# Two quantised feed-forward layers: tokens kept in SBUF, bias rows made in place, ScalarE normalises layer 0, w2a loaded early, new layer 0 orders

## Reference

```python
def layernorm_adapter(x, lang):            # per batch item, weights picked by lang
    h = relu(x @ W1[lang] + b1[lang])      # 256 -> 64
    v = x + h @ W2[lang] + b2[lang]        # 64 -> 256
    n = (v - mean(v)) * rsqrt(var(v) + 1e-5)
    return n * gamma[lang] + beta[lang]
def bitlinear(x, W, b):                    # ternary weights, 8 bit tokens
    ws = clip(mean(|W|), 1e-5); Wq = clip(round(W / ws), -1, 1) * ws
    s = clip(max(|x|, axis=-1), 1e-5);  xq = round(x * 127 / s) * s / 127
    return xq @ Wq.T + b
x = x + bitlinear(gelu(bitlinear(layernorm_adapter(x), W1a, b1a)), W2a, b2a)   # layer 0, 256 -> 1024 -> 256
y = x @ cwl[subject].T + bias[subject]                                         # layer 1
h = depthwise_conv3(bit_linear(y, W1b)) ; x = x + bit_linear(silu(h), W2b)
```

## Time and profile before

| | |
|---|---|
| three runs | 339.78, 340.76, 341.88 us; median 340.76 |
| profiled execution | 339.32 us, span of its trace 337.5 us |
| busy in the span | DVE 290.4 us (86%), PE 271.0 (80%), POOL 268.2 (79%), ACT 222.6 (66%) |
| DMA | 53.12 MB, of it 8.39 MB written to HBM |

### The profile page before, as it was taken

How to read it: one execution, slowest core, us unless ns; L and a number is a source line. 1 busy time by engine, 2 the same in 40 slices (tenths; PEclk the granted TensorE clock), 3 DMA queues, 4 the chain that set the end, 5 groups by cost and what they waited for, 6 DMA issues and landing times.

```text
span 337.5 us, 6487 instructions
## 1 busy us (share of the span) xinstructions
PE 271.0 (80%) x1643; PEld 182.5 (54%) x1668; DVE 290.4 (86%) x635; ACT 222.6 (66%) x339; POOL 268.2 (79%) x443
## 2 busy tenths in 40 slices
PE   5728696897998979899868688897979889686755
PEld 5303353362555546467636467785766667464632
DVE  0427999999999999987699899999999999999651
ACT  4237689897667666562436896778768687777650
POOL 2407999998989898875899899998989899898410
PEclk9875799999799999999989999799999999979995
DMA  7896416696889798568570055667675667267883
GB/s 226 255 338 227 135 35 142 173 192 154 206 177 212 197 252 177 123 147 155 163 223 2 1 125 102 160 155 194 148 187 136 156 149 143 55 155 95 204 139 80
DMA packets 97003, 53.12 MB, mean 157 GB/s; under 512 B 74165, under 2 KB 90301, under 8 KB 96966
## 3 DMA queue, kind: packets, MB, share of 16 engines
q1 hardware_dynamic: 95078, 51.43, 63.5%
q10 hardware_dynamic: 1888, 1.27, 1.4%
HBM read 27.51 MB, written 8.39 MB: 106 GB/s over the span
## 4 chain that ended last, share of the span: by engine, by line
issue 28%; POOL 24%; DVE 23%; PE 13%; DMA 5%; SPq 3%; ACT 2%; DVEq 1%; POOLq 0%
POOL mid L755 7%; PE banks L1197 3%; POOL raw_all L762 3%; DVE amy L969 3%; DMA q1T<-r 3%; POOL xb L735 3%; DVE xb L987 2%; PE banks L1183 2%; DMA raw_all<-in_w2a 2%; PE banks L1314 2%; DVE am L930 2%; DVE raw_all L994 2%; DVE xb L963 2%; DVE zg L899 2%; POOL r L708 2%
## 5 line engine op out<-in xcount | busy, mean ns | idle before, releaser
L762 POOL TENSOR_TENSOR raw_all<-raw_all,mid 128x1024 f32<-128x1024 f32 x32 | 63.6, 1999 | 0.0
L602 ACT ACTIVATE banks<-xb,taps 128x512 f32<-128x512 f32 x64 | 43.6, 689 | 22.9 <-DVE xb L987 22.8
L542 ACT ACTIVATE g<-banks,dqz 128x1024 f32<-128x1024 f32 x32 | 35.4, 1107 | 22.2 <-POOL r L708 18.7
L755 POOL TENSOR_SCALAR mid<-xb,taps,convb 128x512 f32<-128x512 f32 x64 | 48.9, 771 | 0.9 <-DVE xb L987 0.9
L708 POOL TENSOR_SCALAR r<-g,qs 128x1024 uint16<-128x1024 f32 x32 | 36.2, 1133 | 12.1 <-DVE qs L942 12.0
L994 DVE SCALAR_TENSOR_TENSOR raw_all<-xb,taps,banks 128x512 f32<-128x512 f32 x64 | 45.7, 738 | 0.0
L1314 PE MATMUL banks<-tern,q1T 128*128 128x256 bf16 x256 | 35.7, 286 | 10.9 <-DMA q1T<-r 6.1
L987 DVE TENSOR_TENSOR xb<-banks,dqb 128x512 f32<-128x512 f32 x64 | 42.7, 683 | 1.8 <-PE banks L1288 1.8
L1183 PE MATMUL banks<-tern,qT 128*128 128x512 bf16 x117 | 37.4, 395 | 5.1 <-DVE tern L853 3.0
L1288 PE MATMUL banks<-yT,tern 128*128 128x512 bf16 x114 | 32.8, 392 | 9.8 <-DVE raw_all L994 4.8
L1000 DVE TENSOR_REDUCE am<-g 128x1 f32<-128x1024 f32 x32 | 38.8, 1212 | 1.7 <-ACT g L608 1.7
(11 more groups left out here) (113 smaller groups left out, 582.2 us busy)
## 6 DMA issues: line engine op xcount, KB each, us to landing
xr<-in_x SPq DMA_DIRECT2D x8, 512.0 KB, 4.7
x_after_layer<-x SPq DMA_DIRECT2D x16, 256.0 KB, 2.9
x<-x_after_layer SPq DMA_DIRECT2D x8, 512.0 KB, 3.7
xr<-x_after_layer SPq DMA_DIRECT2D x8, 512.0 KB, 3.8
out_y<-o SPq DMA_DIRECT2D x32, 128.0 KB, 2.0
xT<-in_xT SPq DMA_DIRECT2D x4, 512.0 KB, 4.8
x2T<-in_xT SPq DMA_DIRECT2D x4, 512.0 KB, 3.9
wl<-in_cwl SPq DMA_DIRECT2D x8, 256.0 KB, 3.6
```

The lines of the kernel that those rows point to most:

```text
L602: act.activation(bank(BANK_U[g % 3]), apad[:, f, 2:S + 2], ACT.Copy, scale=taps[:, f, 2:3]).then_inc(p_last, 1)
L755: pool.tensor_scalar(mid[f // 2 % 2][:, f % 2, :], apad[:, f, 1:S + 1], taps[:, f, 1:2], convb[:, f:f + 1], ALU.mult, ALU.add).then_inc(p_ ...
L762: pool.tensor_tensor(c[:, 2 * q:2 * q + 2, :], c[:, 2 * q:2 * q + 2, :], mid[q % 2][:, :, :], ALU.add).then_inc(p_sum, 1)
```

## The change

- Tokens stay in SBUF: `xs` holds all 8 items. `load_tokens` writes them there, `residual` adds b2 in place after `add_adapted` has read them, `final1` writes its result in place, layer 1's `transpose_x` and `final2` read it there, `final2` writes the output there, and `store2` sends it. `store1`, the token load of `load2` and `load_residual` are gone, and so are the waits of `final1` and `final2` for stores. `y`, `ry` and `apad` of layer 1 get memory of their own.
- The bias rows: b1 is loaded three times as rows of `b1row`, and ACT and DVE make the three bf16 parts in place (`bias_leading`, `bias_rest`, `bias_middle`, `bias_last`). No DRAM round trip.
- The norm: POOL makes `nratio` = -mean * rstd for a pair, ACT writes `zg` = xx * rstd + nratio (two 256 column Identity activations), and DVE multiplies by gamma and adds beta in one 512 column instruction each (`gain`, `shift`).
- `split_scales` has 4 instructions in place of 7; the transposed scale block `qc` is 128 wide in place of 9.
- `load_weights(1)` is issued before the loads of item 1; `load_weights(2)` and `(3)` go to SP's slot 3; small constants go to the end of SP's opening list; `adapter_in` no longer waits for the load of `cb1`, nor the identities for all constants.
- New orders of layer 0 on all five engines (ACT's, SP's and DVE's shown below).

```diff
+            load_weights(1)
             sp.dma_start(ids_sb[:, B:2 * B], t["ids1"]).then_inc(s_ids, 16)
...
+            def bias_leading():
+                act.wait_ge(s_wsc, 2)
+                act.wait_ge(s_ldb1, 48)
+                act.activation(bias9b[:, :], b1row[:, :], ACT.Copy, scale=iws[:, 0:1]).then_inc(s_b1, 1)
+                act.wait_ge(s_b1, 1)
+                act.activation(b1row[:, :], b1row[:, :], ACT.Copy, scale=iws[:, 0:1]).then_inc(s_b1, 1)
+            def normalise(b, p):
+                act.wait_ge(s_nratio, pair(b, p))
+                wait(act, s_z, pair(b, p - 1))
+                for k in range(2):
+                    ins = act.activation(zg[:, k, :], xx[p][:, k, :], ACT.Identity, scale=rstd[p][:, k:k + 1],
+                                         bias=nratio[p][:, k:k + 1])
+                ins.then_inc(s_norm, 1)
...
+            def negative_ratio(b, p):
+                pool.wait_ge(s_rstd, pair(b, p))
+                pool.wait_ge(s_nmean[p], b + 1)
+                wait(pool, s_norm, pair(b - 1, p))
+                pool.tensor_tensor(nratio[p][:, :], nmean[p][:, :], rstd[p][:, :], ALU.mult).then_inc(s_nratio, 1)
...
             def add_adapted(b, p):
                 dve.wait_ge(s_admm, pair(b, p))
                 dve.wait_ge(s_ldx[b % 2], 16 * (b // 2 + 1))
-                wait(dve, s_zg, pair(b - 1, p))
-                wait(dve, s_ssq, pair(b - 1, p))
+                wait(dve, s_norm, pair(b - 1, p))
...
+            def gain(b, p):
+                dve.wait_ge(s_norm, pair(b, p))
+                dve.wait_ge(s_ldgb[b % 2], 32 * (b // 2 + 1))
+                dve.tensor_tensor(zg[:, :, :], zg[:, :, :], gam[b % 2][:, :].unsqueeze(1).to_broadcast([P, 2, D]),
+                                  ALU.mult).then_inc(s_zg, 1)
+            def shift(b, p):
                 dve.wait_ge(s_zg, pair(b, p))
                 wait(dve, s_rz, pair(b - 1, p))
+                dve.tensor_tensor(z[p][:, :, :], zg[:, :, :], bet[b % 2][:, :].unsqueeze(1).to_broadcast([P, 2, D]),
+                                  ALU.add).then_inc(s_z, 1)
```

More of the change, by code:

```diff
@@ L183, in build_program @@
         s_rz = sem("s_rz")
[L184 removed]
+        s_split = sems("s_split", 3)
         s_qc = sem("s_qc")
@@ L203, in build_program, with tokens @@
         s_colsum = sem("s_colsum")
[L205 to L211, removed]
+        def tokens(b):
+            return xs[:, PAIR * b:PAIR * (b + 1), :, :].rearrange("p n a d -> p (n a) d")
         wl1 = [sb(f"wl1_{k}", [P, KD, D]) for k in range(2)]
@@ L1023, in final2 @@
                                          op0=ALU.mult, op1=ALU.add).then_inc(p_o[k], 1)
             def slot1(s):
-                on(inverse1, s - 3, 2)
+                on(inverse1, s - 3, 1)
+                on(final1, s - 4, 2)
+                on(absmax1, s - 3, 2)
+                once(s, 0, weight_scale, 0)
+                on(inverse_z, s - 2, 1)
+                on(scale1, s - 3, 2)
+                on(gain, s - 1, 0)
+                on(inverse1, s - 3, 2)
+                on(add_adapted, s, 0)
@@ L1027, in slot1 @@
+                on(shift, s - 1, 0)
+                on(negative_mean, s, 0)
+                on(final1, s - 4, 3)
+                once(s, B + 2, linear, 0, 0)
                 on(absmax1, s - 3, 3)
-                on(scale_z, s - 1, 0)
+                once(s, 2, weight_scale, 2)
+                on(absmax_z, s - 1, 0)
                 on(scale1, s - 3, 3)
-                on(add_adapted, s, 0)
-                on(inverse1, s - 3, 3)
-                on(inverse_z, s - 1, 0)
                 on(final1, s - 3, 0)
@@ L1045, in slot1 @@
-                once(s, B + 2, inverse_y, 0)
+                on(absmax1, s - 2, 0)
+                once(s, B + 2, scale_y, 0)
+                on(scale_z, s - 1, 0)
+                once(s, B + 2, inverse_y, 0)
+                on(scale1, s - 2, 0)
+                once(s, 0, bias_rest)
+                once(s, 1, weight_scale, 1)
+                on(inverse_z, s - 1, 0)
+                once(s, 3, weight_scale, 3)
+                on(inverse1, s - 2, 0)
+                on(add_adapted, s, 1)
@@ L1046, in slot1 @@
+                on(gain, s - 1, 1)
                 on(final1, s - 3, 1)
-                on(add_adapted, s, 1)
-                on(inverse1, s - 2, 0)
+                on(shift, s - 1, 1)
+                once(s, 1, ternary, 0)
+                once(s, 0, bias_last)
                 on(absmax1, s - 2, 1)
                 on(absmax_z, s - 1, 1)
-                on(centre, s, 0)
-                on(final1, s - 3, 2)
                 on(scale1, s - 2, 1)
                 on(scale_z, s - 1, 1)
-                on(inverse1, s - 2, 1)
@@ L1056, in slot1 @@
-                on(inverse_z, s - 1, 1)
-                on(absmax1, s - 2, 2)
-                once(s, 1, ternary, 0)
-                on(normalise, s, 0)
-                on(final1, s - 3, 3)
-                once(s, B + 1, linear, 0, 0)
-                on(scale1, s - 2, 2)
-                once(s, 1, weight_scale, 2)
-                on(absmax_z, s, 0)
-                once(s, 0, weight_scale, 1)
             def seam():
```

330 lines of the change are left out of this document (135 added, 195 removed).

## The result

The change makes the kernel slower: median 347.93 us (346.81 to 348.65, four runs) against 340.48 for the kernel before on the same chip, a ratio of 1.022, interval 1.019 to 1.026. I had forecast 327, with 319 to 335 around it. The profiled execution took 347.77 us with a span of 346.0, so 8.5 us more span than the 337.5 of before.

What follows compares the result with a forecast made beforehand. DVE was taken to set the pace in both layers, with PE close behind in layer 0. Gains of 7.5 (start), 1 (slots 2 to 4), 3.7 (full slots) and 1 (tail) took 339.3 to 326.1; median 327, range 319 to 335.

Steps and rivals of the forecast that it cites:

- the part on the norm: Layer 0 slots: four 512 column DVE instructions replace eight of 256, so DVE's slot goes from 15.4 to 14.4 us.
- ACT's cover: Layer 0: four more activations take ACT from 10.3 to 12.1 us of a 14.4 us slot, without lengthening a full slot.
- My price of 496 ns: ACT's two added pairs of 256 column activations a slot, priced by round_z: about 0.9 us a pair, 1.8 a slot.
- POOL's term: Layer 0: nratio adds 0.7 us a slot, split_scales loses as much or more; zero, bounds -0.5 and +0.7.
- Slots 2 to 4: Layer 0 slots where ACT's cover is thin, two holding three weight passes each: together 1 us gained, bounds +3 (lost) and -4.
- DVE's own sum: DVE's layer 0 slot: 15.4 - 0.8 for fewer instructions - 0.2 for fewer collisions = 14.4 us, bounds 13.8 and 15.2.
- Start: First slots: early second weight matrix ends ACT's idle wait, item 2's add_adapted near 35; gain 7.5 us, bounds 3 and 11.
- The rival in which the load only swaps places: First slots: the early matrix delays item 1's adapter as much as it frees ACT; 6 us gained, median 335, chance 0.12.
- PE's floor: Layer 0: slots run at PE's 13.8 us of work; 18.6 us gained in all, median near 322, chance 0.20.
- Layer 1 and the tail: Layer 1's DVE work unchanged; removing a resident load ahead of a late transpose gains 1 us near the end, bounds 0 and 2.
- Tables: ACT: Identity is in every function table set, so normalise adds no table loads and the sum stands.
- The slower rival: Layer 0 on ACT: four 1.28 us table loads a slot, or an order leaving 4 us of waits; 349 us, chance 0.06.

Runs made afterwards that it cites:

- The best kernel: The changed kernel with gamma and beta loads issued earlier, the norm back on DVE, and layer 1's first weight loads at the end of SP's list: 334.26 us, ratio 0.985.
- the run above: The changed kernel with ACT's normalise as Copy with a per-token scale, in place of Identity with scale and bias, mean left out: 343.44 us, one run.

## Why the prediction was wrong

**The step that failed: SP's new order was not walked through.** In the part on the norm I named what stands behind `gain`, and that it waits for ACT. I did not name its other wait, for gamma and beta, although the listing of SP's order stood in front of me with `load_norm s-2` behind the four transposes of the slot before. The sum has no term for it. Of a step that is moved past others on a queue, its landing has to be set against its first use; in the kernel after beta takes 3.2 to 3.9 us to land, and is issued when `gain` is all but due. The runs: moving this pair alone is worth 6.6 us by the ratios and 7.6 by the medians, about all that the change lost against the kernel before.

**ACT's cover.** This is the second step that failed. "It stays under cover in a full slot" holds for ACT's busy time (12.27 us of 18.50 and 15.01 of 19.20, the windows above) and misses the point. What counted was the length of a chain, not room on an engine: rstd, nratio, two activations of 0.59, `gain`. On the old orders it cost `gain` 1.5 us of waiting in each full slot (1.09 and 0.42), and with DVE's other waits it left 0.4 of a saving of 2.4 us on DVE. In the new orders the norm on ACT costs 1.1 to 1.7% of the time. My price of 496 ns was also short by 95. And POOL's term, which I had put at zero for its 2 us of idle time, left out that `nratio` can stand behind POOL's work on the weights: ACT waited 3.46 us for it at 48.13 in the kernel with the norm alone.

**Slots 2 to 4.** I had taken a gain of 1 us with +3 as the bad end. The change lost 4.4 there (4.0, 0.7, -0.2), outside my bounds. With the norm on DVE and early loads the slot from item 2 to item 3 is at 14.5, so this is the thin cover that I named and then didn't believe in: ACT with three weight passes and four more activations.

**DVE's own sum** was right in size: 13.90 and 14.52 us busy against my 14.4. The collisions went on, as forecast: `shift` 985 ns on the average, `gain` 740, where 684 is the free one. That the size came out is in part luck: it depends on the order, and on the old orders, with `shift` at 743, it was 12.9. But busy time is a duration of a slot only while nothing waits, and I turned one into the other.

**Start.** Right in sign and mechanism, short in size: item 2 at 36.96 where I said 35, 5.6 us early and not 7.5. On the kernel before, the early load alone brings item 2 in 2.7 us earlier and is worth 3.1 us to the end; which other part of the change gave the rest was not tried. The rival in which the load only swaps places, with 2 us from the start, doesn't fit the 5.6 us of the change. (My sum of 326.1 and 1.4 is 327.5 and not 327, which changes nothing here.)

**PE's floor** of 13.8 could not be tested by the change. The best kernel's slots are 14.7, with PE at 14.17 of 15.00 in the window, so it leaves little room there.

**Layer 1 and the tail.** Layer 1 is unchanged as forecast (170.9 against 171.5 us, so the tail gave 0.6 at most, where I had said 1). Resident tokens alone gave nothing that can be told from no change (0.998, 0.994 to 1.003).

**Tables.** The trace has no table load in layer 0's slots, only the one of 1.3 us at `silu` and one at the opening of the kernel (L448, 3.55 to 4.83 us), which I had not named. Both were there before. By the rule of the Trainium skill (ScalarE: Activation LUTs, Table sets: the hidden batching unit) Identity is in every set; the trace agrees. The slower rival came out in size, 349 against 347.9, but by none of its table loads; that the number fits is luck. Its second half, an order that leaves 4 us of waits in a slot, is near to what happened in the last two slots (3.8 and 3.1 us longer), and the chance of 0.06 for it was too small, because I had priced the new orders as if an order could only help.

## What to carry over

When orders are rewritten, walk every queue, DMA issues first: for each load, what stands ahead of it, when it lands, and who uses it first; then ask what stands behind that user and whether it leads back to the same queue, since then one late load holds up every engine. Work moved to an idle engine is free only if its result isn't the next thing the busy engine needs: compare the chain that it lengthens with the time that it saves. And where a change has many parts, price each by undoing it alone on both bases; here a good part (early weights), a neutral one (resident tokens), an order that was bad on SP, and a norm in the wrong place made a kernel that is 2% slower, and with the norm and two places on SP put right one that is 1.5% faster.

## What the runs showed of the hardware

- An activation of 128x256 f32 with one per-token operand (`round_z`, `squares`, the Copy step of the run above) takes 492 to 507 ns in these kernels, with two (Identity with scale and bias) 586 to 595.
- A stall is paid for a second time by the matmuls behind it. PE waited 3.20 us until 108.85 in the kernel after; behind the wait the timeline of PE shows eight matmuls of a `down1` at the lower level of the clock, 1.2 GHz, and eight of the same kind, 5 us later, at 2.4. The granted clock of that slot is 0.82, and 1.00 in the two windows of the last experiment, where PE's longest wait is 1.06 us.

```profile
110.69 1.91 PE L1170 MATMUL banks<-tern,q1T 128*128 128x256 bf16 x8
...
115.71 1.04 PE L1170 MATMUL banks<-tern,q1T 128*128 128x256 bf16 x8
```

- A DVE instruction with two SBUF inputs prints longer behind a POOL instruction (1.72 us for a pair at 93.89, with POOL's addition running until 94.92). With other orders and three instructions fewer in `split_scales` the mean of `centre` went from 887 and 838 ns to 581 and 627. The Trainium skill (SBUF — State Buffer, Who interferes with whom) has it that a DVE instruction with two SBUF inputs and a GpSimd instruction that reads SBUF block each other for the whole instruction, whichever issued first going first; the trace agrees, with the pair of 1.72 us that ends after POOL's addition.
- A load issued on SP between transposes: `load2` took SP from 99.45 to about 102 for two DMAs, though their own issues are 0.42 and 0.35 us (1.08 us of it is L385, the reading of the item's number), and the transposes that print alone take 1.25 to 1.27 each. Position on the queue is time.
